# GNN kernel on one core: q made in the layer edge stages, and GpSimd allowed 64 tiles ahead of TensorE

## What is computed

```
h = x @ W_enc.T + b_enc
for l in range(2):
    m = relu(concat[h[row], h[col]] @ msg_W1[l].T + msg_b1[l])
    m = m @ msg_W2[l].T + msg_b2[l]
    agg = segment_sum(m, col, num_segments=N)
    upd = concat[h, agg] @ upd_W[l].T + upd_b[l]
    h = layer_norm(h + upd)
out = layer_norm(x + h @ W_out.T + b_out)
```

## Time and profile before

| | |
|---|---|
| time, median of 3 runs | 3886.1 us (3885.23 to 3891.72) |
| the profiled execution: its own time / its span | 3925.8 us / 3924.1 us |
| PE busy | 3146.7 us (80%) |
| DVE, ACT, POOL busy | 2686.3, 2361.9, 1817.9 us |
| mean granted TensorE clock | 0.93 |
| moved by DMA | 777.83 MB, 198 GB/s over the span |

### The profile page before, as it was taken

One profiled execution on the slowest core, in us unless ns is written; L12 is line 12 of the kernel. 1 busy time (PEld: TensorE's weight loads), 2 busy tenths in 40 slices (PEclk: granted clock), 3 DMA queues, 4 the chain that ended last, 5 costly groups with the idle time before them and its releaser, 6 DMA issues. The chain is left out here.

```text
span 3924.1 us, 93325 instructions
## 1 busy us (share of the span) xinstructions
PE 3146.7 (80%) x25312; PEld 2796.9 (71%) x25312; DVE 2686.3 (68%) x8634; ACT 2361.9 (60%) x5642; POOL 1817.9 (46%) x1782
## 2 busy tenths in 40 slices
PE   4966537766556789978999876999969998778998
PEld 3743326554443379978998776999969988768998
DVE  9999747765436688865666544666647665547998
ACT  3789707655432268875665543566646665436999
POOL 0000133556664533334555564655444555665664
PEclk9989968988778999999999997999989999989999
DMA  0046516765438989995665432899956654426987
GB/s 18 2 143 225 165 38 185 196 173 157 131 100 279 337 294 366 358 331 167 192 187 169 138 110 62 297 323 330 315 190 193 191 173 148 122 72 215 295 295 248
DMA packets 460716, 777.83 MB, mean 198 GB/s; under 512 B 113688, under 2 KB 115864, under 8 KB 460392
## 3 DMA queue, kind: packets, MB, share of 16 engines
q1 hardware_dynamic: 355046, 548.85, 42.3%
q10 hardware_dynamic: 67714, 147.73, 11.0%
q0 software_dynamic: 37632, 77.15, 7.8%
HBM read 451.50 MB, written 321.78 MB: 197 GB/s over the span
## 5 line engine op out<-in xcount | busy, mean ns | idle before, releaser
L885 DVE SCALAR_TENSOR_TENSOR edges_acc<-edges_acc,keep,edges_ps_a 128x128 f32 (+1 forms) x2352 | 820.2, 349 | 374.2 <-remote 121.3
L853 POOL DMA_INDIRECT ring<-table_p,esrc x784 | 760.1, 970 | 640.8 <-PE edges_ps_m L1014 329.8
L1013 PE MATMUL edges_ps_m<-ring,ident 128*128 x3136 | 646.6, 288 | 125.5 <-POOLq L843 50.7
L1014 PE MATMUL edges_ps_m<-edges_q_ring,edges_turned 128*128 x3136 | 632.5, 284 | 27.0 <-issue 26.7
L870 DVE TENSOR_TENSOR edges_onehot<-iota,drel 128x512 f32<-128x512 f16 x441 | 303.6, 689 | 443.5 <-DMA table_p<-nodes_p_out 299.4
L1013 PEld LDWEIGHTS edges_ps_m<-ring,ident 128*128 128x128 f32 x3136 | 499.1, 200 | 148.4 <-issue 98.0
L981 ACT ACTIVATE edges_msg<-edges_ps_m 128x512 f32<-128x512 f32 x392 | 231.4, 590 | 614.3 <-PE edges_ps_m L1014 241.9
L1014 PEld LDWEIGHTS edges_ps_m<-edges_q_ring,edges_turned 128*128 128x128 f32 x3136 | 499.4, 200 | 36.0 <-issue 35.6
L1023 PE MATMUL edges_ps_a<-edges_onehot,edges_msg 128*128 128x128 f32 x3136 | 437.4, 284 | 69.6 <-issue 63.1
L853 POOL DMA_INDIRECT ring<-table_h,esrc x344 | 328.2, 954 | 308.3 <-PE edges_ps_a L1038 157.1
L1023 PEld LDWEIGHTS edges_ps_a<-edges_onehot,edges_msg 128*128 128x128 f32 x3136 | 397.9, 199 | 82.8 <-issue 81.6
(11 more groups left out here) (315 smaller groups left out, 6869.5 us busy)
## 6 DMA issues: line engine op xcount, KB each, us to landing
table_z<-nodes_z_t SPq DMA_DIRECT2D x196, 256.0 KB, 5.0
table_p<-nodes_p_out SPq DMA_DIRECT2D x196, 256.0 KB
table_q<-nodes_q_out ACTq DMA_DIRECT2D x196, 256.0 KB
edges_q_ring<-table_q SPq DMA_DIRECT2D x196, 256.0 KB
edges_d_ring<-table_d ACTq DMA_DIRECT2D x98, 512.0 KB
table_t<-edges_acc SPq DMA_DIRECT2D x196, 256.0 KB
nodes_in_a<-table_t SPq DMA_DIRECT2D x196, 256.0 KB
nodes_in_z<-table_z SPq DMA_DIRECT2D x196, 256.0 KB, 4.5
```

Source lines behind the costliest of these rows:

```text
L853: nc.gpsimd.indirect_dma_start(out=ring[:, e % RE * W:e % RE * W + P], out_offset=None, in_=table[:, :], in_offset=bass.IndirectOffsetOnAx ...
L885: nc.vector.scalar_tensor_tensor(out=to, in0=to, scalar=m.keep[:, s:s + 1], in1=ps_a[:, i % AR, where(j):where(j) + F], op0=ALU.mult, op1= ...
L1013: nc.tensor.matmul(to, m.ident[:], rows[j], start=True, stop=False)
L1014: last = nc.tensor.matmul(to, turned[:, i % QR, j * P:(j + 1) * P], slots[j], start=False, stop=True)
```

## The change

q is no longer made in `nodes` and `nodes0`. The layer edge stage loads z_t again (table_z, 4 buffers `z_in`), makes q on TensorE (`product_q`, L1053 of the changed kernel), and VectorE copies it out of PSUM (`copy_q`): the first 8 chunks straight into `q_ring`, the other 90 into `q_out` (5 buffers), which ScalarE stores to table_q, from where SP loads them into `q_ring` as before. Eight chunks are made ahead of batch 0, and one in each of the batches 0 to 89. AHEAD goes from 24 to 64 in all three edge stages.

```diff
-AHEAD = 24
+AHEAD = 64
+ZR, QO, LEAD = 4, 5, 8
...
+        def load_z(eng, c):
+            if c >= ZR:
+                eng.wait_ge(s_made_q, c - ZR + 1)
+            eng.dma_start(z_in[:, c % ZR, :], m.table_z[layer][turn_back(c) * P:(turn_back(c) + 1) * P, :]).then_inc(s_z[c % ZR], 16)
+        def kept_q(eng, c):
+            eng.wait_ge(s_kept_q[(c - RC) % QO], 16 * ((c - RC) // QO + 1))
+        def copy_q(eng, copy, c):
+            eng.wait_ge(s_made_q, c + 1)
+            if c >= RC + QO:
+                kept_q(eng, c - QO)
+            to = q_ring[:, c * CH:(c + 1) * CH] if c < RC else q_out[:, (c - RC) % QO, :]
+            copy(to, ps_q[:, c % 2, :]).then_inc(s_copied_q, 1)
...
             def _(sp):
                 if not degrees:
-                    for c in range(RC):
-                        sp.dma_start(q_ring[...], chunk(table_q, turn_back(c)))...
-                    sp.wait_ge(s_q_first, 16)
+                    for c in range(LEAD + 2):
+                        load_z(sp, c)
+                    sp.wait_ge(s_copied_q, 1)
...
                         if c + RC < NCHUNK:
+                            kept_q(sp, c + RC)
                             sp.dma_start(q_ring[:, at * CH:(at + 1) * CH], chunk(table_q, turn_back(c + RC))).then_inc(s_q[c % 2], 16)
...
             def _(dve):
+                if not degrees:
+                    for c in range(LEAD):
+                        copy_q(dve, nc.vector.tensor_copy, c)
...
+                    if not degrees and i + LEAD < NCHUNK:
+                        copy_q(dve, nc.vector.tensor_copy, i + LEAD)
...
             def _(act):
+                        if i + LEAD + 2 < NCHUNK:
+                            load_z(act, i + LEAD + 2)
+                        if RC <= i + LEAD - 2 < NCHUNK:
+                            act.wait_ge(s_copied_q, i + LEAD - 1)
+                            act.dma_start(chunk(table_q, turn_back(i + LEAD - 2)), q_out[...])...
...
             def _(pe):
+                def product_q(c):
+                    pe.wait_ge(s_z[c % ZR], 16 * (c // ZR + 1))
+                    if c >= 2:
+                        pe.wait_ge(s_copied_q, c - 1)
+                    for j in range(J):
+                        last = nc.tensor.matmul(ps_q[:, c % 2, j * P:(j + 1) * P], z_in[:, c % ZR, j * P:(j + 1) * P],
+                                                m.wproj[:, layer, D:2 * D], start=True, stop=True)
+                    last.then_inc(s_made_q, 1)
...
                     if i >= BEHIND:
                         segment(i - BEHIND)
+                    if i + LEAD < NCHUNK:
+                        product_q(i + LEAD)
                     if i < NB:
                         combine(i)
...
 (node_stage)
-                    pipelined(act, [(root_y, 2), (copy_z, 4), (norm_y, 3), (evacuate_q, 5), (store_q, 6)])
+                    pipelined(act, [(root_y, 2), (copy_z, 4), (norm_y, 3)])
...
-                            nc.tensor.matmul(part(ps_q, b % 2, j), part(z_t, b, j), m.wproj[:, nxt, D:2 * D], start=True, stop=True)
                             last = nc.tensor.matmul(part(ps_p, b % 2, j), part(z_t, b, j), m.wproj[:, nxt, 0:D], start=True, stop=True)
```

More of the change, by code:

```diff
@@ L764, in _, with edge_stage @@
                 act.wait_ge(s_d, 16)
-def edge_stage(nc, m, table, table_q, agg, degrees, x=None):
+def edge_stage(nc, m, table, table_q, agg, degrees, x=None, layer=None):
     F = P + 1 if degrees else P
@@ L784, in edge_stage @@
             d_ring = sb("d_ring", [P, DR, DB * CH], F16)
-            ps_m = pb("ps_m", 512, QR)
+            ps_m, ps_q = pb("ps_m", 512, QR), pb("ps_q", 512, 2)
+            z_in, q_out = sb("z_in", [P, ZR, CH]), sb("q_out", [P, QO, CH])
+            s_z, s_kept_q = [sem(f"s_z{r}") for r in range(ZR)], [sem(f"s_kept_q{r}") for r in range(QO)]
+            s_made_q, s_copied_q = sem("s_made_q"), sem("s_copied_q")
         else:
@@ L805, in _ @@
                 if not degrees:
-                    for c in range(RC):
-                        sp.dma_start(q_ring[:, c * CH:(c + 1) * CH], chunk(table_q, turn_back(c))).then_inc(s_q[0] if c else s_q_first, 16)
-                    sp.wait_ge(s_q_first, 16)
+                    for c in range(LEAD + 2):
+                        load_z(sp, c)
+                    sp.wait_ge(s_copied_q, 1)
                     sp.sem_inc(s_n, 1)
-                    sp.wait_ge(s_q[0], 16 * (RC - 1))
+                    sp.wait_ge(s_copied_q, RC)
                 sp.sem_inc(s_n, RC if degrees else RC - 1)
@@ L815, in landed @@
                     if not degrees and c + RC < NCHUNK:
-                        sp.wait_ge(s_q[c % 2], 16 * (c // 2 + 1) + (16 * (RC - 1) if c % 2 == 0 else 0))
+                        sp.wait_ge(s_q[c % 2], 16 * (c // 2 + 1))
                     sp.sem_inc(s_n, 1)
@@ L977, in _ @@
                             turn(i + 2)
+                        if i + LEAD + 2 < NCHUNK:
+                            load_z(act, i + LEAD + 2)
+                        if RC <= i + LEAD - 2 < NCHUNK:
+                            act.wait_ge(s_copied_q, i + LEAD - 1)
+                            act.dma_start(chunk(table_q, turn_back(i + LEAD - 2)), q_out[:, (i + LEAD - 2 - RC) % QO, :]).then_inc(s_kept_q[(i + LEAD - 2 - RC) % QO], 16)
                         act.wait_ge(s_pq, i + 1)
@@ L1067, in batch @@
                         segment(i - BEHIND)
+                    if i + LEAD < NCHUNK:
+                        product_q(i + LEAD)
                     if i < NB:
                         combine(i)
+                if not degrees:
+                    for c in range(LEAD):
+                        product_q(c)
                 for i in range(NB + 2):
@@ L1338, in copy_z @@
                     nc.scalar.copy(z_t[:, b, :], ps_t[:, b % 2, :]).then_inc(s_z_t, 1)
-                def evacuate_q(c, b, turn):
-                    act.wait_ge(s_proj, c + 1)
-                    if reused(c, RING):
-                        act.wait_ge(s_store["q"][b], turn * 16)
-                    nc.scalar.copy(q_out[:, b, :], ps_q[:, b % 2, :]).then_inc(s_out_q, 1)
-                def store_q(c, b, turn):
-                    act.wait_ge(s_out_q, c + 1)
-                    act.dma_start(chunk(m.table_q[nxt], c), q_out[:, b, :]).then_inc(s_store["q"][b], 16)
                 root_y = root(mv, rstd, s_aggr, s_std, s_norm)
@@ L1353, in _ @@
                 else:
-                    pipelined(act, [(root_y, 2), (copy_z, 4), (norm_y, 3), (evacuate_q, 5), (store_q, 6)])
-                    for b in range(RING):
-                        act.wait_ge(s_store["q"][b], 16 * slot_uses(RING, b))
+                    pipelined(act, [(root_y, 2), (copy_z, 4), (norm_y, 3)])
             @block.tensor
@@ L1399, in project @@
                     if reused(c, 2):
-                        pe.wait_ge(s_v if final else s_out_q, c - 1)
-                        if not final:
-                            pe.wait_ge(s_out_p, c - 1)
+                        pe.wait_ge(s_v if final else s_out_p, c - 1)
                     for j in range(J):
@@ L1538, in build @@
         for l in range(L):
-            stage(f"edges{l}", edge_stage, m.table_p[l], m.table_q[l], m.table_t, False)
+            stage(f"edges{l}", edge_stage, m.table_p[l], m.table_q[l], m.table_t, False, None, l)
             stage(f"nodes{l}", node_stage, a["x"], out, l)
```

10 lines of the change are left out of this document (5 added, 5 removed).

## The result

The changed kernel takes 4030.9 us (4024.1 to 4037.1, 4 runs) against 3888.0 us of the kernel before on the same chip: ratio 1.037, 95% interval 1.034 to 1.039. It is slower, as forecast, but by 143 us where the forecast of 3947 is 59 above this median. Its profiled execution spans 4035.1 us, 111.0 more than that of before, where the sum said 61. The other 32 us lie in the base: the profiled run of before stood 38 us above its median, that of after 6.

A forecast was written before the change was run, and what follows sets the result against it. TensorE was taken to bound `nodes0` and early edge batches, VectorE `nodes`, with unbroken gather rows holding back hand-overs. Terms: -77 - 14 + 2 x (72 + 40 - 28) - 16 = +61 us, giving 3947 us, range 3845 to 4075.

The forecast's parts named there:

- the tail: End of each layer edge stage: AHEAD 64 frees about 12 more batches from gathers, -28 us (bounds -15 and -35).
- `nodes`: Stage `nodes` loses q, but VectorE stays at 299 us and pays hand-overs: -14 us (bounds -5 and -35).
- Rival B: Layer stage heads: the row of gathers is harmless, head +4 instead of +40, whole kernel 3849 us; chance 0.20.
- rival D: Late layer-stage batches: the longer lead frees them, -85 instead of -28 a stage, whole kernel 3717 us; chance 0.07.
- The forecast's stage: Each layer edge stage: q's products +72, head +40 and tail -28 us.
- AHEAD 64, head of the layer stages: Layer stage heads: the row grows from 24 to 64 gathers and holds other engines, +40 us (bounds 0 and +60).
- Each layer edge stage gains 98 chunks of q: Layer edge stages: 90 products in batches 0 to 89 at +0.80 us each, +72 us (bounds +59 and +120).
- rival C: Layer edge stages: z loads come late, each of 90 products waits 1 us more, whole kernel 4127 us; chance 0.13.
- nodes0 loses q: Stage `nodes0`: q's 88 us of TensorE go, TensorE and DMA both above 90%, 332 us: -77 (bounds -60 and -88).
- degree stage: Degree stage with AHEAD 64: late batches give -29, head and first batches cost about +13: -16 us (bounds -35 and +5).
- The rule against my reading: Skill's rule that DMA never contends with compute engines; if it held, the layer stage heads would cost nothing.

The follow-up runs named there:

- new order: Changed kernel with lead 24, z loaded six products ahead, VectorE's reciprocal (and shift) first and ScalarE's normalisation before its copy in node stages; `nodes0` 329.4 us, ratio 1.012.
- broken-row version: Kernel before with lead 64, GpSimd waiting for landing after each of the first 16 groups of four gathers per layer edge stage; ratio 1.014, `edges0` 729.8 us.
- the ramp: Kernel before, with GpSimd's lead in the layer stages starting at 24 tiles and growing by one tile in six to 44; ratio 1.005, `edges0` 710.5 us.

## Why the prediction was right and wrong

**Right.** The direction; that the row of gathers holds TensorE, VectorE and ScalarE, and the head would cost tens of us (the forecast had the second batch's message 80 us in, the first came at 90.7); that the late batches stay at 4 to 5 us whatever the lead (batches 168 to 180 took 4.7 us each before, 4.3 with the lead of 64 alone and 4.2 in the changed kernel); the tail, forecast at -28 and measured at -30.8 to -32.4; `nodes`, forecast at -14 and measured at -9. Rival B (a harmless row) and rival D (free late batches) are refuted: with the lead alone 72 batches take 255.9 us as before.

**Wrong in size, three terms.** The forecast's stage was +84, the measured +106.7 and +109.7.
- *"AHEAD 64, head of the layer stages", +40:* it measured 55.7, near the bound of 60 and above the 50 us by which the row is longer. I took off 10 us for batches that slip through. With the lead alone only two messages came before the row ended, in the changed kernel none (ScalarE idle for 80.9 us).
- *"Each layer edge stage gains 98 chunks of q", +72:* with q alone `edges0` was 83.9 us longer. A product was priced at 0.80 us and cost 0.88 with q alone (0.92 in the changed kernel). The floor of +0.66 held (3.58 us a batch with z in time, for 2.91 before); the rest, 14.9 us in 72 batches, was z that came late, rival C's cause at a fraction of its price. The wait list named it with 3.8 us only. And the eight products and their copies ahead of batch 0 I had priced as lying in the row; with q alone the first 12 batches took 16.9 us more, where the forecast has 9.6 for the 12 products made in them.
- *"nodes0 loses q", -77:* it gave 56. I compared the busy times of TensorE and of the transfers and took the larger. The bound that appeared was neither (a quarter of the transfers less changed nothing) but the chain from VectorE's moments to TensorE's transposes, whose last wait was 2.6 us before and 23.3 after. With the steps in the new order the stage gives the -80.

In the whole these make 48 us in the two layer edge stages and 21 in `nodes0`; `nodes` adds 5. Against them the degree stage gave 9 more than forecast (its two profiles of before differ by 7), and plan (106.3 to 95.3, a stage that took 91 to 109 us in kernels with the same code there) and conv 15 that belong to no term: luck, which hid part of the miss. Together 50: from 61 to 111.

**The rule against my reading.** The Trainium skill (SBUF — State Buffer, "Who interferes with whom") says that contention comes only from the port pair which VectorE and GpSimd share, and that TensorE and ScalarE wait on nobody. By it the lead would have cost nothing at the head. In the broken-row version TensorE was busy for 7.29 of 51.20 us in a row of gathers and ScalarE idle for 49.29, and in the lead-only version 12 batches took 122.6 us in place of 66.9; the measurement decides. Whether a port has to do with it no run shows, so the page need not be wrong on ports; it does not cover what was seen. What the row holds is not settled: passes and hand-overs come late, and the profile names nothing that they wait behind. Whether the engines' own instructions come late, no run tests.

## What to carry to other kernels

A gather brought forward is not free because GpSimd has time for it: it cost 1.4 us of the stage at the head, in mid-stage and in the ramp, and returned 0.8 where it was missing at the end, so the shorter lead won in the layer stages. Before work is moved off a stage's bounding engine, follow the loop of hand-overs that this engine's time covered; the order of VectorE's and ScalarE's steps was worth 24 us, the transfers nothing. Work that is moved into a stage belongs in the batches that wait for something else, with its loads early; the same products cost 0.88 us in a full batch and nothing in a waiting one.

## What was not expected of the hardware

- Rows of 46 to 64 gathers hold TensorE, VectorE and ScalarE wherever in the stage they stand: copies of VectorE come 20 us apart, ScalarE was idle once for 49.29 us in mid-stage, and TensorE's passes came 2.8 us apart with no wait in the program between them. The granted clock, a mean of the levels 1.2 and 2.4 GHz, is 0.62 to 0.69 in the stretches of 12 batches with such a row, in which TensorE is idle for long, and 0.99 to 1.00 behind them.
- A share of 0.88 to 0.90 of the DMA engines at 282 to 287 GB/s was no limit: once the loads were issued earlier, batches with half the product ran 0.7 us faster each at a share of 0.99 and 343 GB/s, those with the whole product 0.2 us faster at 0.94 and 305 GB/s.
- Taking half of a product's passes away changed little (3.79 and 3.85 us a batch): late z held both at 3.8, above TensorE's own 3.58 and 3.19.
